# The feed-forward stage of a fused attention kernel: group stores and group loads issued in halves

## What is computed

```python
x = x + mlstm_cell(q=ln(x), k=ctx, v=ctx, ...)          # gated linear attention, 4 heads
x = x + ln(x) @ (ternary(w0) * mean|w0|)
x = x + softmax((ln(x) Wq)(ctx Wk)^T / 16) (ctx Wv)
y = act_quant(ln(x))                                    # 127 / max|row|, rounded
h = silu(y @ ternary(w_gate).T) * (y @ ternary(w_up).T) # 256 -> 1024
x = x + act_quant(h) @ ternary(w_down).T                # 1024 -> 256
```

## Time and profile before

| | |
|---|---|
| runs shown | 671.24, 672.07, 674.44 us; median 672.07 |
| the profiled execution | 671.36 us, its span 669.6 us |
| busy: PE, DVE, ACT, POOL | 95%, 85%, 78%, 60% of the span |
| granted clock of PE | 0.999 of full speed |
| group stores (L439) | 15, 505.5 to 663.7 us, landing after 3.3 us (median) |
| group loads (L441) | 12, 506.1 to 637.0 us, landing after 4.8 us (median) |

### The profile page before, as it was taken

The page is one execution under the profiler, slowest core; times in us unless marked ns, Lnnn a source line. Parts: engine busy times, 40 slices in busy tenths (PEclk is TensorE's granted clock), DMA queues, the critical chain, the costliest instruction groups (busy, mean ns, idle before and its releaser), DMA issues.

```text
span 669.6 us, 14974 instructions
## 1 busy us (share of the span) xinstructions
PE 634.2 (95%) x4722; PEld 473.0 (71%) x4722; DVE 566.3 (85%) x1461; ACT 523.6 (78%) x1301; POOL 401.6 (60%) x648
## 2 busy tenths in 40 slices
PE   5889999999999999999999999999899999999996
PEld 4668787787877878778787787877456556555554
DVE  4787879888898888978889788889899899889984
ACT  4666777887878777777777787875789989888985
POOL 3355463554735547356474564653677888787777
PEclk9999999999999999999999999999999999999999
DMA  8310302122121230312203121014245867768673
GB/s 298 113 44 21 95 1 95 49 77 74 42 96 45 83 95 17 96 47 81 96 17 96 48 80 64 17 56 143 64 100 148 178 143 180 138 156 185 148 158 119
DMA packets 105409, 63.64 MB, mean 95 GB/s; under 512 B 52845, under 2 KB 105070, under 8 KB 105334
## 3 DMA queue, kind: packets, MB, share of 16 engines
q1 hardware_dynamic: 98470, 59.29, 33.4%
q10 hardware_dynamic: 6864, 3.41, 1.7%
HBM read 29.39 MB, written 20.97 MB: 75 GB/s over the span
## 4 chain that ended last, share of the span: by engine, by line
PE 62%; DVE 14%; ACT 11%; DMA 6%; issue 3%; SPq 2%; POOL 1%; POOLq 0%; DVEq 0%; ACTq 0%
PE bank L710 11%; PE bank L625 9%; PE bank L678 8%; PE bank L655 8%; DMA us<-usq 6%; PE bank L729 5%; PE bank L699 4%; ACT ew L871 4%; PE bank L530 3%; PE bank L593 3%; ACT x2T L838 2%; PE bank L584 2%; DVE st L1276 2%; PE bank L671 2%; PE bank L575 2%
## 5 line engine op out<-in xcount | busy, mean ns | idle before, releaser
L710 PE MATMUL bank<-WGU,fqT 128*128 128x512 bf16 x512 | 124.9, 380 | 2.5 <-DVE vg L1572 2.0
L1127 POOL TENSOR_SCALAR_AFFINE_SELECT D<-D 128x512 f32<-128x512 f32 x64 | 38.4, 637 | 127.5 <-ACT D L862 127.5
L1572 DVE SCALAR_TENSOR_TENSOR vg<-bank,back,D 128x1024 f32<-128x1024 f32 x64 | 82.0, 1281 | 11.6 <-ACT D L1022 9.2
L710 PEld LDWEIGHTS bank<-WGU,fqT 128*128 128x128 bf16 x512 | 47.0, 98 | 56.7 <-DVE vg L1572 21.4
L1022 ACT ACTIVATE D<-bank,back 128x1024 f32<-128x1024 f32 x64 | 71.5, 1117 | 15.2 <-PE bank L710 15.1
L1579 DVE TENSOR_REDUCE hmax<-vg 128x1 f32<-128x1025 f32 x64 | 78.1, 1221 | 2.2
L1112 POOL TENSOR_TENSOR rs<-ve,minus_half 128x4 f32<-128x4 f32 x64 | 65.3, 1027 | 21.2 <-DVE ve L1282 18.8
L1227 POOL TENSOR_SCALAR wtmp<-vg,hscale 128x1024 f32<-128x1024 f32 x64 | 71.7, 1120 | 5.8
L1276 DVE BATCH_NORM_STATS2 st<-x 128x6 f32<-128x256 f32 x184 | 64.4, 411 | 2.7
L655 PEld LDWEIGHTS bank<-vaug,C 128*128 128x128 f32 x512 | 60.7, 192 | 2.1 <-issue 1.3
L625 PE MATMUL bank<-WX,qcT 128*128 128x268 f32 x256 | 62.0, 395 | 0.0
(11 more groups left out here) (203 smaller groups left out, 1522.1 us busy)
## 6 DMA issues: line engine op xcount, KB each, us to landing
out_dram<-x SPq DMA_DIRECT2D x30, 512.0 KB, 3.3
xg<-in_x_dram SPq DMA_DIRECT2D x16, 512.0 KB, 3.9
cg<-in_ctx_dram SPq DMA_DIRECT2D x16, 512.0 KB, 4.6
xg<-out_dram SPq DMA_DIRECT2D x8, 512.0 KB, 4.8
cg<-out_dram SPq DMA_DIRECT2D x8, 512.0 KB, 5.2
rows_q<-fq ACTq DMA_DIRECT2D x13, 256.0 KB, 2.3
raw<-in_L_ffn_w_gate_dram SPq DMA_DIRECT2D x1, 1024.0 KB, 7.6
nrm<-in_L_ffn_w_up_dram SPq DMA_DIRECT2D x1, 1024.0 KB, 9.6
```

Source lines behind the costliest of these rows:

```text
L710: mm = pe.matmul(ps[k + half], fqT[:, i // 2 % 2, c, i % 2 * P:(i % 2 + 1) * P], WGU[:, c, which, half * 512:(half + 1) * 512], start=(c = ...
L1572: dve.scalar_tensor_tensor(out=fh[i % 2][:, 0:INNER], in0=up, scalar=back[:, i, 1:2], in1=fsil[:, i % 2, :], op0=ALU.mult, op1=ALU.mult).t ...
```

## The change

Each store and each load of a group is split into two of two batches (256 KB each). Half h of group g is stored, and half h of group g + 4 loaded, in iteration i = 4 (g + 2) + 2 h, so at every even i from 8 on; the place in `ffn_block` is the same, behind the product transpose. The store of a half waits for its two sums. The four first loads become eight. Each half has a semaphore of its own, and POOL waits at the first and third batch of a group, each time for the half it needs.

```diff
-        f_in = [sem(f"f_in{p}") for p in range(4)]
-        f_out = [sem(f"f_out{p}") for p in range(2)]
+        f_in = [[sem(f"f_in{p}_{h}") for h in range(2)] for p in range(4)]
+        f_out = [[sem(f"f_out{p}_{h}") for h in range(2)] for p in range(2)]
...
+            def half_in(g, h):
+                some = slice(2 * h, 2 * h + 2)
+                sp.dma_start(fx[g % 4][:, some, :], grp(out, g)[:, some, :]).then_inc(f_in[g % 4][h], 16)
+
             for g in range(4):
-                sp.dma_start(fx[g], grp(out, g)).then_inc(f_in[g], 16)
+                for h in range(2):
+                    half_in(g, h)
             store(NG - 2)
-            def group_out(g):
-                sp.wait_ge(f_done, FB * g + FB)
-                sp.dma_start(grp(out, g), fo[g % 2][:, :, :]).then_inc(f_out[g % 2], 16)
+            def half_out(g, h):
+                some = slice(2 * h, 2 * h + 2)
+                sp.wait_ge(f_done, FB * g + 2 * h + 2)
+                sp.dma_start(grp(out, g)[:, some, :], fo[g % 2][:, some, :]).then_inc(f_out[g % 2][h], 16)
                 if g + 4 < NG:
-                    sp.dma_start(fx[g % 4], grp(out, g + 4)).then_inc(f_in[g % 4], 16)
+                    half_in(g + 4, h)
...
-                if i % FB == 3 and i > 2 * FB:
-                    group_out(i // FB - 2)
+                if i % 2 == 0 and i >= 2 * FB:
+                    half_out(i // FB - 2, i % FB // 2)
...
-            group_out(NG - 2)
+            half_out(NG - 2, 0)
+            half_out(NG - 2, 1)
...
             for p in range(2):
-                sp.wait_ge(f_out[p], 8 * NG + 16 - 16 * p)
+                for h in range(2):
+                    sp.wait_ge(f_out[p][h], 8 * NG + 16 - 16 * p)
...
-                if s == 0:
-                    pool.wait_ge(f_out[g % 2], 8 * (g - g % 2) + 16)
-                    pool.wait_ge(f_in[g % 4], 4 * (g - g % 4) + 16)
+                if s % 2 == 0:
+                    pool.wait_ge(f_out[g % 2][s // 2], 8 * (g - g % 2) + 16)
+                    pool.wait_ge(f_in[g % 4][s // 2], 4 * (g - g % 4) + 16)
...
             for p in range(2):
-                dve.sem_inc(f_out[p], 16)
+                for h in range(2):
+                    dve.sem_inc(f_out[p][h], 16)
```

## The result

The changed kernel takes 667.16 us (median of 6 runs, 666.91 to 669.14), the kernel before 672.22 us (6 runs). The ratio is 0.9928, with a 95% interval of 0.9909 to 0.9947: 4.8 us less, between 3.6 and 6.1 (the two medians by themselves differ by 5.1). Run once more beside other kernels, the changed one gave 0.9930 (0.9917 to 0.9944). The forecast was 668.1 us and 4.0 us less.

The account below looks back on a forecast made before the run. In the feed-forward, one product transpose in four blocks stood behind 1 MB, came about 1 us late and stopped TensorE and ScalarE. 6.0 - 0.4 - 1.0 - 0.6 = 4.0 us off 672.07 gave 668.1; range 666.1 to 672.6.

Parts of the forecast that it names:

- The forecast case: Feed-forward stage: ScalarE's waits for late product transposes fall from 7.9 to under 1.5 us, saving 4.0 us; chance 0.58.
- The ceiling, 6.0 us: Feed-forward blocks 16 to 60: at the unhindered pace 125.7 us instead of 131.7, so at most 6.0 us saved.
- What is late next, 0.4 + 1.0 us: Last three groups' single-row work: 0.4 us already visible stays, and 1.0 more is charged where DMA waits had covered it.
- ring: Feed-forward's gate, silu, multiply, up across engines: small waits, TensorE on VectorE 14.3 us, VectorE on ScalarE 7.8.
- Late transposes without a cause, 0.6 us: Product transposes late with no store or load explaining it now and then meet a half pair: 0.6 us charged.
- The sum: Whole kernel: 6.0 - 0.4 - 1.0 - 0.6 = 4.0 us saved.
- The row transpose and the odd transpose: SP's queue behind a half pair: row transpose costs nothing; odd product transpose 0.3 us late with 1.8 spare, no stall.
- The store at 490.07: A 512 KB store in the old trace, in a half pair's position; row and odd transposes behind landed in 3.0 and 2.4 us.
- SP's work: SP's issuing in the feed-forward: 5.15 us per two blocks against 5.71 needed, so 0.5 us in hand.
- SP becomes the bound: Rival: held-up DMA issues raise SP to 6.2 us per two blocks, 5 us slower, 677; chance 0.05.
- The added waits, nothing: SP's waits for two GpSimd sums per half and GpSimd's two extra semaphore waits per four blocks cost nothing.
- A transfer costs by its number: Rival: a half pair delays what follows in SP's queue by a full pair's 3.3 us, giving 680; chance 0.05.

Follow-up runs that it names:

- runs with few bytes: Kernel before, its group stores and later group loads cut to 16 of 256 columns: 667.79 us; the same cut in the changed kernel: 667.41 us.
- half pairs of few bytes: Changed kernel, its half stores and half loads beyond the four first groups cut to 16 of 256 columns: 667.41 us, ratio 0.9912 to the kernel before.
- both halves in the old place: Changed kernel with both half pairs one behind the other at i = 11, 15, ..., ahead of an even product transpose: 677.99 us, ratio 1.0077 to the kernel before.
- the quarters: Changed kernel split further, one batch (128 KB) stored and one loaded in every block from 8 on: 684.21 us, ratio 1.0163 to the kernel before.
- The half pairs at odd blocks: Changed kernel with its half pairs at odd i from 9 on, directly ahead of the next even product transpose: 667.01 us, ratio 0.9921 to the kernel before.
- the two runs that tell them apart: Kernel before, whole groups in the old place, only the stores or only the loads cut to 16 of 256 columns: 669.44 and 667.43 us respectively.

## Why the prediction was right

The forecast case came in, and by its own mechanism. Point by point:

- **The ceiling, 6.0 us.** The pace of blocks 60 to 63 (2.857 us) was taken for the whole stretch. The runs with few bytes put the floor at 126.5 us, or 2.875 a block, so 5.2 us were to be had. The other 0.8 is the price of the next term.
- **What is late next, 0.4 + 1.0 us.** Over-charged: row work and ring together cost 126.5 - 125.7 = 0.8 us. Its mechanism is right and can be seen in block 28.
- **Late transposes without a cause, 0.6 us.** The size came out, by luck; the mechanism did not. There is one wait of 0.2 us in the trace. The 0.6 us between the changed kernel and the floor lie almost wholly in blocks 21 to 24, which take 12.2 us, and 11.5 both in the kernel before and in its run with few bytes. Lost cover can't be the reason, since that run has no waits that could give any; with half pairs of few bytes the four take 11.9 us. What lengthens them stays open.
- **The sum.** 4.0 forecast; 4.6 in the stretch, 4.8 by the ratio. The difference in the stretch is the one term of row work, 1.4 where it was 0.8.
- **The row transpose and the odd transpose.** The store at 490.07 was a good stand-in, as it had the bytes, the place and the neighbours of a half pair. The bound for the odd one (0.3 us late, 1.8 to spare) held: 2.4 to 2.5 us. The delay was not cut to half, as the bound had it, but to less, so the bound was a safe one. "The row transpose costs nothing" held here, but not by itself: with both halves in the old place and late issue it became the one that everyone waited for.
- **SP's work.** 5.15 us per two blocks forecast, 5.07 measured, of 5.78 that two blocks take. That would leave 0.7 us; the held-up issues take a part of it, and SP's list of waits has 6.9 us for ScalarE's result between 503 and 650 us, about 0.3 per two blocks. So there is something in hand, but less than the 0.5 that was forecast, and the quarters use it up. The rival "SP becomes the bound" came one halving too early: it had asked for 0.84 us of hold-up in every pair, and all hold-ups of the stretch come to 7.2 us, 0.3 a pair. Its row of 2.26 us was not the traffic's work either: with few bytes the issue at the same place, 554.0, takes 1.97.
- **The added waits, nothing.** The profile's list of SP's waits puts 7.3 us in 17 places between 503 and 650 us down to the sums of GpSimd, which looks like a miss. The timeline above says otherwise: the store at 514.49 begins 0.05 us after the issue ahead of it ends at 514.44, and so it is with every half store up to 650 us. The half pairs at odd blocks have 0.2 us of this wait and the same time.
- **A transfer costs by its number.** Fell with the few bytes (no wait) and with both halves in the old place (678, not 690). The Trainium skill's rule to batch DMAs to 1 MiB ("DMA: Bandwidth & Descriptors", "Measured") is about bandwidth, and this stage wants a short queue. The halves do land sooner, by less than half: the store after 2.3 us where it was 3.3, the load after 3.0 to 3.4 where it was 4.8. The fit of the Trainium skill, "DMA: Bandwidth & Descriptors", "Anatomy of one DMA", is for another issuing path and would give, as an estimate, 2.6 against 3.2 for either; the measured difference is larger for both, most of all for the load.

```profile
out_dram<-x SPq DMA_DIRECT2D x30, 256.0 KB, 2.3
xg<-out_dram SPq DMA_DIRECT2D x16, 256.0 KB, 3.0
cg<-out_dram SPq DMA_DIRECT2D x16, 256.0 KB, 3.4
```

## What to carry to other kernels

Where small, urgent transfers share a queue with large ones that nobody waits for, ask for each urgent one how long after its issue it is wanted, and cut or spread the large ones until what stands ahead fits into that. Then count the issuing engine's time per round before cutting further: one more halving turned a gain of 0.7% into a loss of 1.6%. Look for a place in the old trace where a transfer of the new size already stands in the new position; it tells more than any rule.

## What was not expected of the hardware

A load of 512 KB from DRAM delays the transpose behind it in the same queue far more than a store of 512 KB to DRAM: medians of 4.4 against 2.8 us in the two runs that tell them apart, where the transpose alone lands after 2.5. Why the two differ was not tried.

And the issue of a DMA transpose on SP is not a fixed 1.19 us. Directly behind a whole pair it takes 1.4 to 1.5 us. Now and then it is held much longer, up to 3.85 us, which delays everything that SP has yet to issue. This is not the traffic of the groups alone, since the changed kernel with few bytes has it too; SP's timeline, and the list of DMA queues between 567 and 571 us:

```profile
567.69 2.56 SPq L426 DMA_TRANSPOSE fqT<-rows_q  x1
```

```profile
q8 instruction: 1, 0.02, 2.3%
```

The second line is one transfer of 16 KB on the queue that the profile names after instructions. Over the 14 traces, between 503 and 660 us, 83 of the 84 issues on SP that took more than 1.55 us lie within 1 us of such a transfer, and only 205 of the 1635 others. The 3.85 us at 572.54 have one at 573.2, the transposes at 554 one between 554 and 556, and the late one of the earlier trace rows, issued at 608.67, one at 609.8. So the long hold-ups go together with the loading of instructions; which of the two brings about the other, or what both, was not tried.
